# Two recurrences of an eigenvector stage: one product of each step written on GpSimd instead of VectorE

## The reference, cut to what matters

```python
L = jnp.diag(deg) - A
L_norm = d_inv_sqrt[:, None] * L * d_inv_sqrt[None, :]
_, U = jnp.linalg.eigh(L_norm)
agg = jnp.einsum('mn,bnd->bmd', U.T, features)
h = jax.nn.relu(agg @ W1 + b1)
out = h @ W2 + b2
return jnp.einsum('nm,bmd->bnd', U, out)
```

## Time and profile before

| | us |
|---|---|
| median of 3 runs | 9074.54 |
| lowest and highest run | 9060.8, 9084.09 |
| the profiled execution, its own time | 9050.87 |
| its span, from the first instruction to the last | 9048.8 |
| VectorE busy | 6694.3 (74%) |
| GpSimd busy | 1213.5 (13%) |

### The profile page before, as it was taken

The page is one execution under the profiler, slowest core; times in us unless marked ns, Lnnn a source line. Parts: engine busy times, 40 slices in busy tenths (PEclk is TensorE's granted clock), DMA queues, the critical chain, the costliest instruction groups (busy, mean ns, idle before and its releaser), DMA issues. The chain is left out here.

```text
span 9048.8 us, 333441 instructions
## 1 busy us (share of the span) xinstructions
PE 5619.6 (62%) x138898; PEld 3811.5 (42%) x138898; DVE 6694.3 (74%) x32749; ACT 2714.4 (30%) x7811; POOL 1213.5 (13%) x5408
## 2 busy tenths in 40 slices
PE   5696888777788878777776555344433430046956
PEld 2364555555566666666565544011000000033446
DVE  3566666677777777887888888888888889954055
ACT  1442111111111111111113344566666640011046
POOL 0000111121222222222223333000000000000000
PEclk8898999999999999998775555555555555578989
DMA  1000000000000000000000000000000000000000
GB/s 38 1 1 20 4 4 4 4 4 4 4 4 4 4 4 4 4 4 4 4 4 4 4 4 4 0 0 0 0 0 0 0 0 0 0 0 1 0 19 19
DMA packets 24626, 42.17 MB, mean 5 GB/s; under 512 B 2464, under 2 KB 20128, under 8 KB 23200
## 3 DMA queue, kind: packets, MB, share of 16 engines
q1 hardware_dynamic: 23200, 21.70, 0.8%
HBM read 17.50 MB, written 4.19 MB: 2 GB/s over the span
## 5 line engine op out<-in xcount | busy, mean ns | idle before, releaser
L331 PE MATMUL tri_y<-L 128*32 128x256 f32 (+7 forms) x36792 | 1915.5, 337 | 18.6 <-issue 10.1
L331 PEld LDWEIGHTS tri_y<-L 128*32 128x32 f32 x36792 | 1157.3, 119 | 251.7 <-issue 44.6
L441 ACT ACTIVATE tri_mu<-tri_ring,tri_tiny 128x1 f32<-128x1 f32 x990 | 258.8, 261 | 1872.1 <-PE tri_ring L295 1872.1
L1605 PE MATMUL ev_pairs<-ev_sgn,ident 128*128 128x448 bf16 x1024 | 428.5, 573 | 580.3 <-ACT ev_sgn L1570 580.3
L1729 DVE SCALAR_TENSOR_TENSOR ev_seq<-ev_seq,ev_rowG,ev_u 128x112 f32<-128x112 f32 x2048 | 682.8, 333 | 90.7 <-DVE ev_u L1714 2.0
L444 ACT ACTIVATE tri_sM<-tri_half_M,tri_s 128x8 f32<-128x8 f32 (+5 forms) x767 | 228.6, 298 | 1435.4 <-DVE tri_s L661 1435.4
L1714 DVE TENSOR_TENSOR ev_u<-ev_shifted,ev_seq 128x112 f32<-128x112 f32 x2048 | 560.5, 274 | 86.9 <-DVE ev_seq L1736 14.3
L1559 ACT ACTIVATE ev_shifted<-ev_x,ev_rowG 128x112 f32<-128x112 f32 x2112 | 613.2, 373 | 31.4 <-DVE ev_rowG L1686 31.4
L295 PE MATMUL tri_ring<-L 128*32 128x32 f32 (+25 forms) x35704 | 596.1, 205 | 1.2 <-issue 1.1
L295 PE MATMUL tri_k<-tri_kp,tri_half 128*32 128x1 f32 x6136 | 190.0, 183 | 631.5 <-DVE tri_x L670 630.0
L295 PEld LDWEIGHTS tri_ring<-L 128*32 128x32 f32 x35704 | 512.1, 117 | 1.4 <-issue 1.4
(11 more groups left out here) (667 smaller groups left out, 14129.8 us busy)
## 6 DMA issues: line engine op xcount, KB each, us to landing
adj<-in_adj_dram SPq DMA_DIRECT2D x12, 1024.0 KB, 8.1
x<-in_x_dram SPq DMA_DIRECT2D x8, 512.0 KB, 7.2
out_dram<-x SPq DMA_DIRECT2D x8, 512.0 KB, 6.6
gcn_w<-in_L_gnn_W_dram SPq DMA_DIRECT2D x2, 128.0 KB, 2.2
spec_w<-in_L_gnn_W_dram SPq DMA_DIRECT2D x2, 64.0 KB, 2.0
dot_wt<-in_L_gnn_W_dram SPq DMA_DIRECT2D x1, 64.0 KB, 1.7
dot_rows<-in_L_gnn_b_lin_dram SPq DMA_DIRECT2D x1, 64.0 KB, 2.7
dot_rows<-in_L_gnn_b_dram SPq DMA_DIRECT2D x1, 64.0 KB, 3.8
```

The costliest lines, as they stand in the source:

```text
L331: last = nc.tensor.matmul(y[32 * g:32 * g + 32, 0:T * 32], A[:, b + t, XC:XC + 1].broadcast_to([P, 32]), cols, start=(t == 0), stop=(t == ...
L441: nc.scalar.activation(mu[:, :], sigma, ACT.Sqrt, bias=tiny[:, :]).then_inc(root_ready, 1)
L1605: last = nc.tensor.matmul(sums[h], S["ident16"][:, :], sgn[:, h * (GRP // 2) + k:(h + 1) * (GRP // 2) + k, :].rearrange("p s w -> p (s w)" ...
```

## The change

In each step of the segments' recurrence VectorE makes `gB` for the first start vector alone (128 x 512 in place of 128 x 1024), and GpSimd makes the other half. In each step of the rows' recurrence GpSimd makes the product that was L2040 and puts it into `VB`, which is free by then, in two halves that alternate. GpSimd waits on `chain` for the sum of two steps before, in `rot_done` and `row_done`, and raises a new semaphore, `pool_part`, for which VectorE's sum waits. GpSimd's part of the block stands behind VectorE's in the code, since it uses the counts that VectorE's part writes down.

```diff
                 for s in range(1, SEG):
                     gB = (gB0, gB1)[s % 2]
-                    mark(V.tensor_tensor(gB, everywhere(c_[:, s, :]), rot[:, (s - 1) % 3], ALU.mult))
+                    rot_done[rnd, s] = k_old
+                    mark(V.tensor_tensor(gB[:, 0], lanes(c_[:, s, :]), rot[:, (s - 1) % 3, 0], ALU.mult))
                     after(k)
                     k1 = mark(V.tensor_tensor(gA, both(R_[:, s, :, :]), rot[:, s % 3], ALU.mult))
                     after(k1)
+                    parts += 1
+                    dve.wait_ge(pool_part, parts)
+                    k_old = k
                     k = mark(V.tensor_tensor(rot[:, (s + 1) % 3], gA, gB, ALU.add))
...
                     after(k2)
-                    mark(V.tensor_tensor(t2[:, :, :], lanes(c_[:, e + 1, :]), E_[:, e + 1], ALU.mult))
+                    row_done[rnd, s] = k2_old
                     m2_ = mark(V.tensor_tensor(t4[:, :, :], R_[:, e], E_[:, e], ALU.mult))
                     after(m1_)
                     k1 = mark(V.tensor_tensor(D_[:, s + 1], t1[:, :, :], t3[:, :, :], ALU.add))
                     after(m2_)
-                    k2 = mark(V.tensor_tensor(E_[:, e - 1], t2[:, :, :], t4[:, :, :], ALU.add))
+                    parts += 1
+                    dve.wait_ge(pool_part, parts)
+                    k2_old = k2
+                    k2 = mark(V.tensor_tensor(E_[:, e - 1], VB[:, s % 2], t4[:, :, :], ALU.add))
...
+            for rnd in range(2):
+                for s in range(1, SEG):
+                    pool.wait_ge(chain, rot_done[rnd, s])
+                    nc.gpsimd.tensor_tensor((gB0, gB1)[s % 2][:, 1], lanes(c_[:, s, :]), rot[:, (s - 1) % 3, 1], ALU.mult).then_inc(pool_part, 1)
+                for s in range(1, SEG - 1):
+                    e = SEG - 1 - s
+                    pool.wait_ge(chain, row_done[rnd, s])
+                    nc.gpsimd.tensor_tensor(VB[:, s % 2], lanes(c_[:, e + 1, :]), E_[:, e + 1], ALU.mult).then_inc(pool_part, 1)
```

More of the change, by code:

```diff
@@ L1823, in eigenvectors @@
         eS = sb("eS", [P, J]); thr = sb("thr", [P, J]); m1 = sb("m1", [P, 4]); prodS = sb("prodS", [P, 16]); one16 = sb("one16", [P, 16])
-        chain, tables, gamma_ready, abs_ready, right_ready, right_scaled, z_ready, norm_ready, root_ready, factor_ready, scaled = map(
-            sem, ("chain", "tables", "gamma_ready", "abs_ready", "right_ready", "right_scaled", "z_ready", "norm_ready", "root_ready", "factor_ready", "scaled"))
+        chain, tables, gamma_ready, abs_ready, right_ready, right_scaled, z_ready, norm_ready, root_ready, factor_ready, scaled, pool_part = map(
+            sem, ("chain", "tables", "gamma_ready", "abs_ready", "right_ready", "right_scaled", "z_ready", "norm_ready", "root_ready", "factor_ready", "scaled", "pool_part"))
         block = ctx.enter_context(nc.Block())
+        rot_done, row_done = {}, {}
         row = lambda a, t: a[:, :, t, :]
         natural = lambda t: Y[:, t, :].rearrange("p (j s) -> p s j", s=SEG)
[L1830 to L1836, removed]
         @block.scalar
@@ L1873, in _ @@
             V = nc.vector
+            parts = 0
             link(V.memset(one16[:, :], 1.0))
@@ L1928, in _ @@
                 after(k)
-                k = mark(V.tensor_copy(rot[:, 1, 0, :, :], R_[:, 0, :, :]))
+                k = k_old = mark(V.tensor_copy(rot[:, 1, 0, :, :], R_[:, 0, :, :]))
                 for s in range(1, SEG):
                     gB = (gB0, gB1)[s % 2]
-                    mark(V.tensor_tensor(gB, everywhere(c_[:, s, :]), rot[:, (s - 1) % 3], ALU.mult))
+                    rot_done[rnd, s] = k_old
+                    mark(V.tensor_tensor(gB[:, 0], lanes(c_[:, s, :]), rot[:, (s - 1) % 3, 0], ALU.mult))
                     after(k)
@@ L2032, in _ @@
                 after(k2)
-                k2 = mark(V.tensor_tensor(E_[:, SEG - 2], E_[:, SEG - 2], bB, ALU.add))
+                k2 = k2_old = mark(V.tensor_tensor(E_[:, SEG - 2], E_[:, SEG - 2], bB, ALU.add))
                 for s in range(1, SEG - 1):
@@ L2145, in _ @@
             dve.wait_ge(scaled, NT)
+        @block.gpsimd
+        def _(pool):
+            nc.gpsimd.iota(rev[:, :, :], pattern=[[-1, SEG], [-SEG, J]], base=N, channel_multiplier=0, allow_small_or_imprecise_dtypes=True).then_inc(tables, 1)
+            nc.gpsimd.iota(crow[:, :], pattern=[[-SEG, J + 1]], base=N, channel_multiplier=0, allow_small_or_imprecise_dtypes=True).then_inc(tables, 1)
+            nc.gpsimd.memset(muF[:, :, :], 1.0).then_inc(tables, 1)
+            nc.gpsimd.memset(muB[:, :, :], 1.0).then_inc(tables, 1)
+            lanes = lambda a: a.unsqueeze(1).broadcast_to([P, NT, J])
+            for rnd in range(2):
[6 more added lines that the diff above has]
+                    nc.gpsimd.tensor_tensor(VB[:, s % 2], lanes(c_[:, e + 1, :]), E_[:, e + 1], ALU.mult).then_inc(pool_part, 1)
 def program(nc, x, adj, prm, out):
```

## The result

The changed kernel takes 9099.12 us (median of 20 runs, 9079.85 to 9113.89) and the kernel before 9069.09 us (median of 20 runs, 9053.28 to 9085.54). The ratio is 1.0032, with a 95% interval of 1.0024 to 1.0039: 30 us slower. The forecast was 27 us slower and 9101. The ratios in this document are estimates from all runs and not quotients of the two medians; they differ from those by up to 0.0007.

A forecast was written before the change was run, and what follows sets the result against it. VectorE's instructions, one behind the other, were taken to bound the two recurrences. 59.7 us of standing against 33.0 saved gave 26.7 us slower, 9074.5 + 26.7 = 9101.2 us, with a range of 9056 to 9124.

The forecast's parts named there:

- The mechanism: In both recurrences, while a GpSimd product reads SBUF, a VectorE instruction with two SBUF inputs stands: 1.03 us per product.
- What bounds the kernel: In both recurrences VectorE's instructions, one behind the other, are the path: VectorE is busy for 560.33 of the block's 580 us.
- What VectorE is spared: Halved product in the segments' recurrence, 30 times, 16.1 us; product gone from the rows' recurrence, 28 times, 16.9; together 33.0.
- GpSimd in time: In both recurrences GpSimd has over a step of about 3 us for 1.1 us of work; VectorE should not wait.
- The extra semaphore: A second semaphore on a VectorE instruction that waited already: costed at nothing, at most 0.11 us, 58 times, 6 us.
- GpSimd's length: GpSimd's product of 512 elements, carried on from small ones, was to take 1067 to 1139 ns.
- The stop: VectorE's standing for each GpSimd product in both recurrences: 0.99 + 0.04 = 1.03 us, 58 times, 59.7 us.
- The four meetings: In `tridiagonalise`, L667 beside GpSimd's L285 took 0.17, 0.17, 0.23 and 0.19 us, read as VectorE standing some 0.08 us.
- The copy beside the table: A copy of 64 elements, usually 0.22 us, took 0.74 while GpSimd wrote a table for 1.05; cited as a similar case.
- wide instructions run freely beside each other: Rival for both recurrences: only small instructions stop at their start, nothing is added, 9041.5 us, faster by 0.36%; chance 0.13.
- they share a rate: Rival: VectorE runs slower or stands partly while GpSimd reads, 0.3 to 0.7 us a product, 9059 to 9082; chance 0.12.
- The serial rival: GpSimd enters only at VectorE's wait or holds VectorE off throughout: 29 to 39.5 us slower, 9103.6 to 9114; chance 0.17.

The follow-up runs named there:

- the kernel with the fills: The changed kernel with each of GpSimd's 58 products replaced by a fill of the same 512 elements that reads nothing from SBUF: ratio 0.9956, 9022.06 us.
- the kernel with PSUM and the later start: The changed kernel with c and the products with R in PSUM, GpSimd held back until VectorE's last product of the step before: ratio 0.9968, 9036.7 us.

## Why the prediction was right

**The number.** The mechanism was right, and so was its size, 1.07 us a product against 1.03. That 9101 lies only 2 us from the 9099 measured is partly luck: the forecast was added to a median of three runs, 9074.5, and twenty runs of the same kernel give 9069.1. The difference itself was forecast 3.3 us too small, 26.7 against 30.0. The prediction held that 0.3% could hardly be told from none; with twenty runs of each the interval is 1.0024 to 1.0039, and it can.

**What bounds the kernel** held. VectorE had next to no idle time in the loops, and each 0.5 us of a step stood in the time.

**What VectorE is spared**, 33.0 us, was right: 32.4 us came off when GpSimd wrote without reading.

**GpSimd in time** held, in all steps but the first of each rows' recurrence. There VectorE stood at the new wait for 1.2 us, twice, the 2.4 us of the groups above. The extra semaphore, costed at nothing, cost next to nothing, as the kernel with the fills shows.

**GpSimd's length was mis-sized.** I carried 1.71 to 1.86 ns an element from arrays of up to 24 on to 512 and got 1067 to 1139 ns. Undisturbed it takes 1.26 us. The "GPSIMD Engine Reference" of the Trainium skill (Performance versus the Vector engine), from which I had estimated about 1.2, was nearer. In the change it lasted 1.64, the 0.38 more being its own standing until the running VectorE product had read its inputs.

**The stop** was the disputed term: 1.03 us expected, 1.06 to 1.07 measured. So the mechanism read from the earlier trace rows, two small instructions that met in another stage, carried over to arrays more than twenty times as wide. The four meetings stand for many: between 1807 and 2507 us of the trace before, L667 started 0.01 to 0.10 us behind L285 thirteen times, and the eight that started 0.01 to 0.06 us behind were stretched, to 0.18 to 0.23 us. Where it began first, it kept its 0.17. The copy beside the table is no witness, though: that GpSimd instruction only wrote, and GpSimd's fills stopped no product here. What stretched the copy to 0.74 us no run here tells.

The working of the 1.03 was a little off in two ways that cancelled, and that is luck: the slope is 2.1 ns an element and not 1.86, and there is hardly a fixed part, neither my 0.08 us at 21 elements nor the 0.04 for lost overlap. A step of 4.02 and one of 4.05 us were forecast, 4.06 and 4.07 came.

**The rivals.** That wide instructions run freely beside each other and that they share a rate are excluded: each time one instruction ran at its usual speed and one stood. The serial rival, in which GpSimd comes in only at VectorE's wait or holds VectorE off from its start to its end, is not excluded by the price: its 1.07 us and its 29 us slower are as near to what was measured as the forecast is. It is excluded in the steady steps by the order of time. VectorE has no idle time there, and L1930 had 1.22 us left to run at 7465.82 + 2.28 - 1.22 = 7466.88, while GpSimd's product ended at 7467.02: VectorE stood for 1.06 us of the 1.64 that GpSimd's instruction was open. Its first form appeared once in each rows' recurrence, where GpSimd came in only when VectorE stood at the wait:

```profile
7573.78 4.67 POOL L2165 TENSOR_TENSOR vec_VB<-ne2p,Em 128x512 f32<-128x512 f32 x2 [66.13 <-DVE Em L2032]
7574.22 0.68 DVE L2037 TENSOR_TENSOR vec_t<-UT,Dm 128x512 f32<-128x512 f32 x1
7574.82 0.69 DVE L2040 TENSOR_TENSOR vec_t<-UT,Em 128x512 f32<-128x512 f32 x1
7575.42 0.68 DVE L2042 TENSOR_TENSOR Dm<-vec_t 128x512 f32<-128x512 f32 x1
7577.33 1.66 DVE L2047 TENSOR_TENSOR Em<-vec_VB,vec_t 128x512 f32<-128x512 f32 x1 [1.22 <-POOL vec_VB L2165]
```

Three VectorE instructions go by without a stop while GpSimd's first product is open, and VectorE then stands for 1.22 us with nothing to do. The 66 us for which GpSimd had been idle are not the reason. In the kernel with PSUM and the later start the same product, after 63.62 us of idleness, met an instruction with one SBUF input, got in at once and took its usual time:

```profile
7553.54 0.68 DVE L2042 TENSOR_TENSOR vec_t<-vec_cP,Dm 128x512 f32<-128x512 f32 x1
7553.70 1.27 POOL L2171 TENSOR_TENSOR vec_VB<-ne2p,Em 128x512 f32<-128x512 f32 x1 [63.62 <-DVE Em L2038]
```

So it is VectorE's two-input instructions that kept it out. Why they did so for three instructions there, and for one from the second step on, no run told apart, and it stays open.

The rule of the Trainium skill ("SBUF — State Buffer", section "Who interferes with whom") agrees with the runs on who stops whom: a GpSimd instruction that only writes stopped nobody (two fills of 0.99 us beside products that kept their 0.69), one that reads stopped VectorE's two-input instructions in full (1.06 us), and VectorE instructions with one SBUF input kept their 0.68 and 1.22 us. That whoever issues first holds the other off fits the steady steps, but not the first product of each rows' recurrence, which three VectorE instructions passed.

## What to carry to other kernels

Work moved from VectorE to GpSimd is no gift where both read SBUF: as long as GpSimd reads, a VectorE instruction with two SBUF inputs stands, and here each element moved cost 2.1 ns and saved 1.05. Before such a move, look for a stretch of VectorE instructions with at most one SBUF input, long enough for the GpSimd instruction, and set the semaphore so that it falls into it; idle PSUM can make such a stretch. Here the meetings of two small instructions elsewhere in the trace, at several offsets, were enough to see that they shut each other out; the rate per element had to come from wide ones (2.1 ns measured against the 1.86 carried over).

## What the runs showed that I had not expected

- A two-input product on GpSimd takes 1.26 us for 512 f32 numbers per partition, and the reading in it stops VectorE for 1.06; a fill takes 0.52 and a copy's reading stops VectorE for 0.41.
- The stop has next to no fixed part: 0.53 us at 256 elements, 1.06 at 512.
- Moving one operand of VectorE's `tensor_tensor` and the result of another to PSUM left their lengths as they were, 0.67 to 0.69 and 1.21 to 1.22 us.
